# Half of the copies of the transposed source moved from VectorE to ScalarE in a four-layer image kernel

## The reference

```python
def deform_block(x, ow, ob, dw, pw, pb, K):      # one third of the channels, K = 3, 5, 7
    offsets = conv2d(x, ow, ob, K // 2)           # 2*K*K maps of offsets
    # for each of the K*K taps: sample x bilinearly at grid + tap + offset,
    # times the tap's weight for the channel, added up
    out = deform_depthwise(x, offsets, dw, K, K // 2)
    return conv2d(out, pw, pb, 0)                 # pointwise sums over channels

out = concatenate([deform_block(c3, ..., 3), deform_block(c5, ..., 5), deform_block(c7, ..., 7)])
return out * se_weight(out, fc1_w, fc2_w)
```

## Time and profile before

| | us |
|---|---|
| median of three runs | 6244.67 |
| the three runs | 6222.61, 6245.45, 6244.67 |
| profiled execution, device time | 6233.4 |
| its span in the trace | 6231.6 |
| granted TensorE clock, mean | 0.96 of full |
| deformable stages | about 1990 to 5235 of the span |

### The profile page before, as it was taken

The page is one execution under the profiler, slowest core; times in us unless marked ns, Lnnn a source line. Parts: engine busy times, 40 slices in busy tenths (PEclk is TensorE's granted clock), DMA queues, the critical chain, the costliest instruction groups (busy, mean ns, idle before and its releaser), DMA issues. The chain is left out here.

```text
span 6231.6 us, 119455 instructions
## 1 busy us (share of the span) xinstructions
PE 5593.8 (90%) x45628; PEld 3921.1 (63%) x45628; DVE 4793.5 (77%) x10108; ACT 3896.2 (63%) x5359; POOL 610.0 (10%) x772
## 2 busy tenths in 40 slices
PE   5999999999976998999989999899998996999798
PEld 2555454554533557885568875678755885655688
DVE  5888888888875789897789887898878997334333
ACT  3767776776761557885577866688855995211232
POOL 2111111211102102001011000110100000000000
PEclk9999999999998999999999999999999998999898
DMA  4221221221214445555455545455644565111798
GB/s 148 65 55 48 71 63 45 67 61 46 61 40 118 114 110 127 123 121 139 107 128 117 126 116 139 109 130 122 137 112 115 126 143 144 41 41 41 172 236 195
DMA packets 196238, 656.95 MB, mean 105 GB/s; under 512 B 62742, under 2 KB 64590, under 8 KB 152960
## 3 DMA queue, kind: packets, MB, share of 16 engines
q1 hardware_dynamic: 171312, 598.49, 39.3%
q0 software_dynamic: 24320, 50.37, 3.3%
HBM read 535.84 MB, written 62.15 MB: 96 GB/s over the span
## 5 line engine op out<-in xcount | busy, mean ns | idle before, releaser
L2439 PE MATMUL b_near_p<-b_near_work,b_near_hkt 64*128 64x144 f32 (+37 forms) x27520 | 2094.7, 307 | 245.2 <-DVE b_near_acc L2311 148.6
L2439 PEld LDWEIGHTS b_near_p<-b_near_work,b_near_hkt 64*128 64x128 f32 x27520 | 1948.7, 193 | 451.3 <-DVE b_near_work L2384 252.5
L2384 DVE TENSOR_TENSOR b_near_work<-b_near_work 128x140 f32<-128x140 f32 (+26 forms) x5312 | 1583.1, 349 | 215.3 <-PE b_near_p L2439 119.8
L2282 ACT ACTIVATE b_near_work<-b_near_work,b_near_mcol 128x512 f32<-128x512 f32 (+6 forms) x1328 | 765.1, 647 | 866.1 <-DVE b_near_work L2384 696.0
L2286 ACT ACTIVATE b_near_work<-b_near_work,b_near_mrow 128x544 f32<-128x544 f32 (+6 forms) x1328 | 762.4, 645 | 0.0
L539 ACT ACTIVATE a_ex<-a_p_t 128x1024 f32<-128x1024 f32 x512 | 524.2, 1024 | 364.4 <-PE a_p_t L477 363.3
L2311 DVE SCALAR_TENSOR_TENSOR b_near_acc<-b_near_p,b_near_dwc,b_near_acc 128x323 f32<-128x323 f32 (+14 forms) x1088 | 622.8, 575 | 156.8 <-PE b_near_p L2439 153.2
L614 DVE TENSOR_REDUCE a_nm<-a_p_x 128x1 f16<-128x1024 f32 x512 | 625.6, 1222 | 149.8 <-PE a_p_x L466 143.0
L1816 PE MATMUL b_near_p<-b_near_hp,b_near_ow 128*98 128x480 f32 (+14 forms) x1568 | 652.5, 566 | 0.0
L620 DVE TENSOR_TENSOR a_el<-a_ex,a_eh 128x1024 f16<-128x1024 f32 x512 | 621.8, 1214 | 8.0 <-ACT a_eh L544 7.0
L544 ACT CAST a_eh<-a_ex 128x1024 f16<-128x1024 f32 x512 | 535.4, 1046 | 50.8
(11 more groups left out here) (225 smaller groups left out, 5448.0 us busy)
## 6 DMA issues: line engine op xcount, KB each, us to landing
b_near_work<-sampling_positions_near SPq DMA_DIRECT2D x664, 512.0 KB, 6.6
d_win<-merged_kernels SPq DMA_DIRECT2D x192, 263.0 KB, 6.8
b_near_xin<-x SPq DMA_DIRECT2D x21, 1024.0 KB, 8.9
a_xr<-in_x SPq DMA_DIRECT2D x12, 1536.0 KB, 6.6
a_xh<-in_x SPq DMA_DIRECT2D x9, 1536.0 KB, 6.4
x<-a_xr SPq DMA_DIRECT2D x9, 1536.0 KB, 5.7
b_near_xr<-x SPq DMA_DIRECT2D x13, 1024.0 KB, 15.3
x<-b_near_xr SPq DMA_DIRECT2D x13, 1024.0 KB, 4.7
```

Of the source, the lines that this page charges most:

```text
L2282: last = e.activation(rx[:, u, xo[c]:xo[c + 1]].rearrange("p (a b) -> p a b", a=H), pp[:, b, 1, :].rearrange("p (a b) -> p a b", a=H)[:, : ...
L2384: e.tensor_tensor(S[:, k % NS, 0:(r1 - r0) * w].rearrange("p (a b) -> p a b", b=w), rx[:, u, xo[cc]:xo[cc + 1]].rearrange("p (a b) -> p a ...
L2439: last = e.matmul(G[:, a0 - top:z0 - top, c0 - left:c1 - left], hkt[64 * s:64 * s + 64, SIDE * cr + cc, :], S[64 * s:64 * s + 64, k % NS, ...
```

## The change

In each of the twelve stages the copies of groups 2 and 3 of the transposes leave VectorE and are made by ScalarE, as activations with the function Copy and the scale 1 or -1. They stand on ScalarE's list behind the hats of tap 0 and in front of the sums of the stage before. VectorE keeps groups 0 and 1. Both signal the same semaphores as before.

```diff
             def scalar(e):
...
                     e.activation(ry[:, u, 0:yo[TURNED]], ry[:, u, 0:yo[TURNED]], ACT.Relu, bias=1.0, scale=-1.0).then_inc(tp.s_ry.sem, 1)
                     if tap == 0:
+                        for j in range(2, 4):
+                            filled(e, us[j])
+                            e.activation(hkt[:, 4 * j:4 * j + 4, :], bank_of(us[j][1]).rearrange("p (i c) -> p i c", c=P), ACT.Copy,
+                                         scale=-1.0 if j >= TURNED else 1.0).then_inc(s_cu[us[j][1]].sem, 1)
                         take_sums(e, gp, stage)
...
             def vector(e):
...
-                for j in range(4):
+                for j in range(2):
                     filled(e, us[j])
                     part = bank_of(us[j][1]).rearrange("p (i c) -> p i c", c=P)
                     e.tensor_scalar(hkt[:, 4 * j:4 * j + 4, :], part, -1.0 if j >= TURNED else 1.0, None, ALU.mult).then_inc(s_cu[us[j][1]].sem, 1)
```

## The result

The changed kernel takes 6246.67 us, the kernel before 6232.42 us (medians of 12 runs each): +14.25 us, ratio 1.0023 with a 95% interval of 1.0014 to 1.0033, so 9 to 21 us slower. Its profiled execution has a span of 6247.2 us, 15.6 us more than that of before.

The account below looks back on a forecast made before the run. TensorE was taken to set the pace at the stage heads, its queue at the idle ones. Terms 13.1 + 5.1 + 1.0 = +19.2 us gave 6252.6 or 6263.9 by base; forecast 6258, range 6235 to 6279.

Parts of the forecast that it names:

- The new wait: At four 5x5 heads, TensorE's convolution steps wait for bank 0's copy, queued behind tap 0's hats on ScalarE: 13.1 us.
- The clock: Behind the 5x5 stalls, TensorE's clock falls to half speed: three falls of four, 3 x 1.7 = 5.1 us.
- The seven idle heads: 3x3 heads of pairs 2 to 4 and all 7x7 heads: copies fit ScalarE's idle time, 0 us, at most 2.
- The first 3x3 head: First 3x3 stage: copies follow the hats, delaying sampling matmuls and tap 1's hats; 1.0 us, between 0.2 and 1.3.
- The sum: Whole kernel: stalls, clock falls and first 3x3 head together, 13.1 + 5.1 + 1.0 = +19.2 us.
- Rivals 1 to 4: Long low clock, 6268-6279 us (0.12); 5x5 stall hidden, 6233-6247 (0.08); VectorE bounds heads, 6223-6234 (0.05); table loads, 6265-6290 (0.02).
- the fourth: Each stage pays two activation table loads, 31 us in all, partly hidden at idle heads; 6265 to 6290, chance 0.02.

## Why the prediction was right, point by point

**The new wait.** Right. It is at the four 5x5 heads, it is the convolution steps that wait, and the wait is for group 2's copy behind the hats; moving group 3 alone costs nothing, moving group 2 alone costs 12 us, and taking the copies ahead of the hats removes it. The size was forecast start to start as 13.1 us; counted from the end of the sums it is the 11.1 us of idle time and 4 x 0.16 us of overlap that the steps had with the sums, 11.8. TensorE moves 0.63 us after the copy's start, not 0.72 (0.4 us over four heads); most of the rest is that ScalarE started the hats earlier, 10.7 us behind the first transposes at the four heads together instead of 11.9. That differs between executions and was not forecast. Nor is the stall absorbed later: in the middle of each 5x5 stage TensorE waits 3.30 us for VectorE, and this wait ends 163.47, 163.51, 163.48 and 163.70 us behind the first transpose before, and 167.75, 166.19, 168.15 and 166.68 us in the change. Of the 15.0 us that the heads lost, 14.6 are still there. The 0.72 us that the Trainium skill's page "ScalarE: Activation LUTs" (Rules for kernel authors) gives for such an activation as an estimate is too much for this one: the trace has 0.589 us as the mean of all 24, and 1.05 us for two in a row, which overlap.

**The clock.** Right as a mechanism, too large as a term: two falls of four in the profile and 7.57 - 6.15 + 7.81 - 6.15 = 3.1 us, against three falls and 5.1. The odds came from waits in sparser work, eleven of twelve; here they were four of twelve. One reading of the rows was also inexact: in eight of those eleven the low stretch begins 0.3 to 1.3 us before the end of the wait, not at its end or behind it. The prediction took from the Trainium skill's page "TensorE: Matmul & The Clock Gate" (HAM oscillation) that idle gaps drop the clock, and from it a fall at each of the four. The page makes it depend on how long TensorE is idle, which that sentence left out, so the page does not give four falls. The runs have four of twelve at stalls of 2.45 to 3.10 us, and four of four at 4.70 us and over.

**The seven idle heads at nothing.** Borne out by the profiles: 0.27 us of cover left at the head shown, 3x3 stages of 98.1 us before and after. In the runs up to 9 us remain possible.

**The first 3x3 head.** Forecast 1.0 us, measured 2.3. The copies' part is 0.9 us: a later batch of convolution steps starts 21.79 us behind the first transpose (1994.91) instead of 20.92 (1990.65). The first sampling matmul comes no later (6.88 us behind the first transpose, 6.89 before), where 0.2 us had been forecast. Most of the rest is the clock: that batch takes 7.76 us instead of 6.54, and the granted clock is 0.51 over 6.9 us around its start, instead of 0.50 over 3.4. First after, then before, TensorE's timeline:

```profile
2015.57 1.21 PE L2443 MATMUL b_near_p<-b_near_work,b_near_hkt 64*128 64x132 f32 x8 [2.10 <-DVE b_near_acc L2315]
2016.70 7.76 PE L1816 MATMUL b_near_p<-b_near_hp,b_near_ow 128*98 128x377 f32 x14
```

```profile
2010.59 1.05 PE L2439 MATMUL b_near_p<-b_near_work,b_near_hkt 64*128 64x132 f32 x8 [2.12 <-DVE b_near_acc L2311]
2011.57 6.54 PE L1816 MATMUL b_near_p<-b_near_hp,b_near_ow 128*98 128x377 f32 x14
```

**The sum.** The terms as measured in the profile are 11.8 + 3.1 + 2.3 = 17.2 us against 19.2, and the runs say 14.25, between 9 and 21. That the two profiles differ by nearly as much, 15.6 us of span, is partly luck: in the changed one the first deformable stage starts 4.3 us later (1994.91 against 1990.65), from there to the start of the last stage it takes 19.4 us more, and from that start to the end of the kernel 8.0 us less. The 4.3 us and the 8.0 us are scatter of layers that the change does not touch (the last stage itself is 0.3 us longer). The forecast of 6258 was 11 us high, and half of that is the base: it stood halfway between the profiled execution, 6233.4, and the median of three runs, 6244.67, and over 12 runs the kernel before takes 6232.42. The profiled execution was the better base. The 0.5% (31 us) that the prediction gave as what a measurement can tell was too much: over 12 runs the interval is 6 us to either side, and the change is clear of no change. Rivals 1 to 4 did not happen (the fourth counts eight idle heads where there are seven, which changes nothing): no stage shows a table load for the copy, a slowing of about 3 us behind a stall of this size came once in twelve, in the kernel with the change in the 5x5 stages alone, and VectorE's earlier start at the idle heads was lost in a wait.

**What a single stage tells.** I had forecast 3 to 5 us for each 5x5 stage. They grew by 4.3, 7.4, 2.6 and 2.4 us, so three of the four miss it. The second grew by 4.7 us more than its head; most of this arises in its last 8 us. Windows there and in the first 3x3 stage, after and before:

```profile
2015.00:2021.90 6.90, 6.33 (x16) 3.39 (x17) 5.44 (x17) 2.73 (x6) 0.37 (x1) 0.51 1.05 255
3213.10:3226.80 13.70, 9.09 (x51) 7.67 (x49) 12.91 (x21) 2.03 (x3) 6.48 (x4) 0.50 0.30 69
```

```profile
2010.80:2014.20 3.40, 3.40 (x12) 1.84 (x11) 3.40 (x10) 2.47 (x4) 0.76 (x1) 0.50 1.09 320
3198.60:3205.50 6.90, 6.27 (x41) 5.37 (x38) 6.58 (x16) 1.70 (x2) 6.83 (x5) 0.51 0.69 147
```

The low stretch that begins near the end of the second 5x5 stage is 13.7 us long after and 6.9 before. The kernel with group 3 alone moved has the heads of before and still 5x5 stages of 292.2, 292.8, 290.7 and 285.9 us, where before has 289.5, 287.9, 287.4 and 285.8, and it costs nothing over 11 runs. With the change in the first 3x3 stage alone the third 5x5 stage takes 293.5 us, where before has 287.4. So single 5x5 stages differ by up to 6 us between executions without any cause at their heads, and what differs in the windows is where the low clock falls. The 3x3 heads repeat to 0.1 us and the 5x5 heads with the copies of before to 0.3 us (12.71 to 12.97); the 7x7 heads do not, as shown above. For an effect of 3 us in a stage of 290, the head is to be read, not the stage. The four 5x5 stages together do separate, though not by exactly what their heads lose: 1164.3 to 1167.6 us in the three profiles with the stall of the change, 1150.6 to 1161.6 us in the six with the heads of before. The kernel with the stall filled has 1177.1 us in its one profile, 10 us more than the change, which its runs do not show.

## What to carry to other kernels

When an engine takes over a copy out of a bank, ask who writes that bank next, and where the copy stands in the new engine's list: the writer now waits for all that is ahead of it there. ScalarE at 63% busy had plenty of room; at the 5x5 heads it had none at the moment that counted. Relieve an engine only of the work that another waits for (here the first two copies, not the last two), and place it ahead of what is itself waiting for data. The gain of this is 1.0 to 1.2 us a head here, 7 to 12 us of 6235.

## What the runs showed of the hardware

A stall of TensorE can cost more than its length. Behind stalls of 4.7 to 5.6 us the same convolution steps took 7.6 to 9.0 us instead of 6.1, and once 9.11 behind a stall of 2.88 us; behind eight of the twelve stalls of 2.45 to 3.10 us they took 6.15. With the stall filled by useless matmuls they stayed at 6.1. ScalarE's plain copy of 128x512 f32 out of a bank takes 0.57 to 0.60 us (two in a row 1.05, as they overlap; 0.60 each after idle time), where VectorE's takes 0.68 to 0.69 in the mean; so the moved copy was no dearer on the new engine.
